# Fetching four active adapters by register-offset transfers instead of selecting them by matmuls

## The reference, cut to what matters

```
y = einsum('bth,oh->bto', x, W_base) + b_base
A = lora_A[active]                                   # 4 of 16, each 8 x 1024
Bm = lora_B[active]                                  # 4 of 16, each 1024 x 8
z = einsum('bth,erh->bter', x, A)
contribs = einsum('bter,eor->bteo', z, Bm) * SCALING
logits = (einsum('bth,eh->bte', x, router_W) + router_b)[..., active]
alpha = softmax(log(domain_prior[active] + EPS) + logits)
return y + einsum('bteo,bte->bto', contribs, alpha)
```

## Time and profile before

| | |
|---|---|
| median of 3 runs | 1496.22 us (1495.15 to 1497.36) |
| the profiled execution | 1493.93 us |
| its span | 1492.1 us |
| granted TensorE clock, mean | 0.998 |
| busy: PE, DVE, ACT, POOL | 98%, 67%, 48%, 31% |
| DMA queue of SyncE | 144.96 MB, 35.9% of 16 engines |

### The profile page before, as it was taken

One profiled execution on the slowest core, in us unless ns is written; L12 is line 12 of the kernel. 1 busy time (PEld: TensorE's weight loads), 2 busy tenths in 40 slices (PEclk: granted clock), 3 DMA queues, 4 the chain that ended last, 5 costly groups with the idle time before them and its releaser, 6 DMA issues.

```text
span 1492.1 us, 28269 instructions
## 1 busy us (share of the span) xinstructions
PE 1465.0 (98%) x9647; PEld 1376.2 (92%) x9647; DVE 994.3 (67%) x2367; ACT 722.3 (48%) x1618; POOL 462.1 (31%) x537
## 2 busy tenths in 40 slices
PE   6999999999999999999999999999999999999999
PEld 4889898989988988898879999999999999999998
DVE  8756576666565655555676777677677677677674
ACT  5544455545544444554444454454454454454452
POOL 3133233223323323332412332332332332332230
PEclk9999999999999999999999999999999999999999
DMA  6443423442342343234423334334324324324322
GB/s 133 112 104 106 115 79 92 113 114 86 85 113 71 99 113 99 77 106 112 139 101 100 89 80 112 90 79 112 94 75 112 96 72 112 97 72 112 99 70 71
DMA packets 54644, 145.99 MB, mean 98 GB/s; under 512 B 17265, under 2 KB 19761, under 8 KB 54594
## 3 DMA queue, kind: packets, MB, share of 16 engines
q1 hardware_dynamic: 53904, 144.96, 35.9%
q10 hardware_dynamic: 690, 0.37, 0.1%
HBM read 111.75 MB, written 33.55 MB: 97 GB/s over the span
## 4 chain that ended last, share of the span: by engine, by line
PE 94%; DVE 3%; issue 1%; DMA 0%; POOL 0%; ACT 0%; SPq 0%; POOLq 0%; DVEq 0%; ACTq 0%
PE bank L1579 48%; PE bank L1406 13%; PE bank L1408 13%; PE bank L1407 13%; PE bank L1739 4%; PE bank L1611 1%; PE bank L1600 1%; PE bank L1644 1%; PE bank L1673 0%; DMA ends<-in_x_dram 0%; DVE win L1144 0%; DVE mtmp L1143 0%; PE bank L1756 0%; PE bank L1662 0%; DVE fw_l L1138 0%
## 5 line engine op out<-in xcount | busy, mean ns | idle before, releaser
L1579 PE MATMUL bank<-fw_h,ct_h 128*128 128x354 f32 (+2 forms) x1256 | 448.9, 357 | 0.8 <-DVE xout L1109 0.8
L1579 PE MATMUL bank<-fw_l,ct_h 128*128 128x354 f32 (+2 forms) x1256 | 444.9, 354 | 0.0
L1579 PE MATMUL bank<-fw_h,ct_l 128*128 128x354 f32 (+2 forms) x1256 | 443.2, 353 | 0.0
L401 POOL COPY conv_buf<-edge 128x4 f32 (+1 forms) x128 | 21.6, 197 | 852.5 <-DVE tw L1240 838.6
L1579 PEld LDWEIGHTS bank<-fw_h,ct_l 128*128 128x128 f32 x1256 | 236.3, 188 | 21.4
L1579 PEld LDWEIGHTS bank<-fw_h,ct_h 128*128 128x128 f32 x1256 | 236.8, 189 | 17.7 <-DVE ct_l L1264 0.9
L1579 PEld LDWEIGHTS bank<-fw_l,ct_h 128*128 128x128 f32 x1256 | 236.8, 189 | 15.5
L392 POOL TENSOR_TENSOR d_l<-d_f,d_h 128x512 fp32r<-128x512 f32 x128 | 154.9, 1210 | 106.2 <-ACT d_h L605 106.1
L1406 PE MATMUL bank<-d_h,tw 128*128 128x256 f32 x640 | 181.5, 284 | 0.3 <-DVE beta L945 0.3
L386 POOL TENSOR_TENSOR d_f<-xraw 128x512 f32<-128x512 f32 x128 | 170.0, 1351 | 35.1 <-DMA xraw<-in_x_dram 19.2
L1408 PE MATMUL bank<-d_h,tw 128*128 128x256 f32 x640 | 180.7, 282 | 0.0
(11 more groups left out here) (254 smaller groups left out, 3128.9 us busy)
## 6 DMA issues: line engine op xcount, KB each, us to landing
xraw<-in_x_dram SPq DMA_DIRECT2D x32, 512.0 KB, 6.5
xres<-in_x_dram SPq DMA_DIRECT2D x32, 512.0 KB, 4.3
x_dram<-xout SPq DMA_DIRECT2D x32, 512.0 KB, 3.0
xraw<-x_dram SPq DMA_DIRECT2D x32, 512.0 KB, 6.5
xres<-x_dram SPq DMA_DIRECT2D x32, 512.0 KB, 4.4
xraw<-in_x_dram SPq DMA_DIRECT2D x32, 511.5 KB, 7.8
xraw<-x_dram SPq DMA_DIRECT2D x32, 511.5 KB, 7.9
out_dram<-xout SPq DMA_DIRECT2D x31, 512.0 KB, 2.9
```

What stands on the lines that cost most here:

```text
L1579: last = mm(ffn_ps[e][:, 0:cols.stop - cols.start], ctf((ct_h, ct_h, ct_l)[part], k), (fw_h, fw_l, fw_h)[part][:, k, cols], start=k == beg ...
```

## The change

The indices are clamped as before and also written as integers (`act_c`, step 5). At the turns of pairs 9 to 12 (`GATHER` = 9), SyncE reads one index each into a register and issues three transfers with that register as offset: the expert's A (8 rows of `a_in`), its router row (a ninth kind of row, `a_in` rows 32 to 35), and its B (64 columns of `b_in`, 1024 pieces of 32 bytes). The loads of all sixteen A, B and router rows go. Step 15 on TensorE keeps the small product `lsum` and has eight transposes of the 36 gathered rows; step 16 has eight transposes of B, which VectorE packs three times over at step 15 (`prep_pack`). `sel`, `prep_b_turn`, `prep_b_turned` and `prep_between` go; `prep_rows` on VectorE moves from step 17 to 16 and `prep_base` from 16 to 17. In layer 1 the turn of pair 2 moves into the loop.

```
 def load_lora():
     for dst, src in ((act_i[:, :], a["L1_ffn_active"].unsqueeze(0).broadcast_to([P, E_ACT])),
-                     (a_in, a["L1_ffn_lora_A"].rearrange("e r h -> (e r) h")),
-                     (b_in, a["L1_ffn_lora_B"].rearrange("e (p g) r -> p e g r", g=CHUNKS)),
                      (rb_in[:, :], a["L1_ffn_router_b"].unsqueeze(1)),
                      (pr_in[:, :], a["L1_ffn_domain_prior"].unsqueeze(1))):
         sp.dma_start(dst, src).then_inc(zs["lora_in"], 16)
+
+def gather(e):
+    sp.wait_ge(zs["chosen_ready"], 1)
+    v = sp.value_load(act_c[0:1, e:e + 1], min_val=0, max_val=E_TOT - 1)
+    sp.dma_start(a_in[R * e:R * e + R, :], a["L1_ffn_lora_A"][bass.ds(v, 1)].rearrange("o r h -> (o r) h")
+                 ).then_inc(zs["gathered"], 16)
+    sp.dma_start(a_in[ZR + e:ZR + e + 1, :], a["L1_ffn_router_W"][bass.ds(v, 1)]).then_inc(zs["gathered"], 16)
+    sp.dma_start(b_in[:, 64 * e:64 * e + 64].rearrange("p (g r) -> p g r", g=CHUNKS),
+                 a["L1_ffn_lora_B"][bass.ds(v, 1)].rearrange("o (g p) r -> (o p) g r", g=CHUNKS)
+                 ).then_inc(zs["gathered"], 16)
...
-turn(2, not n)
-if not n:
-    load_lora()
-with sp.Fori(3, NPAIR) as j:
-    turn(j)
+if n:
+    with sp.Fori(2, NPAIR) as j:
+        turn(j)
+else:
+    turn(2, True)
+    load_lora()
+    with sp.Fori(3, GATHER) as j:
+        turn(j)
+    for e in range(E_ACT):
+        turn(GATHER + e)
+        gather(e)
+    with sp.Fori(GATHER + E_ACT, NPAIR) as j:
+        turn(j)
...
-nc.scalar.dma_start(r_in, a["L1_ffn_router_W"]).then_inc(zs["lora_late"], 16)
...
 def prep_pack():
-    dve.wait_ge(zs["lora_in"], 16 * 5)
-    v.tensor_copy(b_pack, b_in.rearrange("p e g r -> p g e r")).then_inc(zs["pack_ready"], 1)
+    dve.wait_ge(zs["gathered"], 16 * 3 * E_ACT)
+    for i in range(3):
+        last = v.tensor_copy(b_pack[:, :, i, :, :], b_in.rearrange("p (e g r) -> p g e r", e=E_ACT, g=CHUNKS))
+    last.then_inc(zs["pack_ready"], 1)
...
 def prep_base(link):
-    dve.wait_ge(zs["lora_late"], 32)
+    dve.wait_ge(zs["lora_late"], 16)
+    dve.wait_ge(zs["bb_acc"], 1)
...
+def prep_rows():
+    pe.wait_ge(zs["sel_ready"], 1)
+    pe.wait_ge(zs["gathered"], 16 * 3 * E_ACT)
+    mm(bank[6][:, 256:256 + E_ACT], lsum[:, :], sel16[:, :], start=True, stop=True)
+    for k in range(CHUNKS):
+        pos = slice(256 * (k // 2) + k % 2, 256 * (k // 2) + 256, 2)
+        last = nc.tensor.transpose(bank[7][:, 64 * k:64 * k + NZ], a_in[:, pos], ident[0:NZ, 0:NZ])
+    last.then_inc(zs["ar_acc"], 1)
...
 def prep_b_rows():
     pe.wait_ge(zs["ar_ready"], 1)
-    for g in range(2):
-        last = mm(bank[6 + g][0:96, :], sel[:, :, :, :].rearrange("p g e r -> p (g e r)"),
-                  b_t[:, 512 * g:512 * g + 512], start=True, stop=True)
+    pe.wait_ge(zs["pack_ready"], 1)
+    for g in range(CHUNKS):
+        last = nc.tensor.transpose(bank[6 + g // 4][0:3 * ZR, (g % 4) * P:(g % 4 + 1) * P],
+                                   b_part[:, 3 * ZR * g:3 * ZR * g + 3 * ZR], ident[:, :])
     last.then_inc(zs["bb_acc"], 1)
```

More of the change, by code:

```diff
@@ L52 @@
 PREP, PREPS = 2, 20
+GATHER = PREP + 7
 def half(p):
@@ L199, in build @@
         act_m = sb("act_m", [P, E_ACT])
[L200 to L205, removed]
+        act_c = sb("act_c", [P, E_ACT], I32)
+        pidx_i = sb("pidx_i", [P, 1], I32)
+        pidx = sb("pidx", [P, 1])
         sel16 = sb("sel16", [E_TOT, E_ACT])
@@ L213, in build @@
         b_part = win[1][:, 0:L]
-        b_pack = b_part.rearrange("p (g e r) -> p g e r", g=CHUNKS, e=E_TOT)
+        b_pack = b_part[:, 0:CHUNKS * 3 * ZR].rearrange("p (g i e r) -> p g i e r", g=CHUNKS, i=3, e=E_ACT)
         f_rows = [f_in[0], f_in[1], xres, xout]
-        a_in, r_in, bias_in = f_in[0][:, :], win[0][0:E_TOT, 0:L], win[0][96:97, 0:L]
-        b_in = f_in[1][:, :].rearrange("p (e g r) -> p e g r", e=E_TOT, g=CHUNKS)
-        b_t = f_in[1]
+        a_in, bias_in = f_in[0][0:NZ, :], win[0][96:97, 0:L]
+        b_in = f_in[1][:, 0:E_ACT * CHUNKS * R]
         gate = sb("gate", [P, 16])
@@ L249, in build @@
         zs = {k: sem(k) for k in (
[L250 removed]
+            "f_load0 f_load1 f_load2 f_load3 style_load style_acc pack_ready lora_in ident_made bias_row_moved ln_in ln_ready sel_ready chosen_ready gathered ar_acc "
             "ct_rest wk_side st_made down_made scales_made lora_late ar_ready bb_acc bb_ready z_acc logit_ready exp_ready zcat_ready zt_acc zt_ready gate_step sta_zero").split()}
@@ L367, in _ @@
             nc.gpsimd.iota(pidx_i[:, 0:1], [[0, 1]], base=0, channel_multiplier=1).then_inc(zs["ident_made"], 1)
-            nc.gpsimd.iota(rr_i[:, :, :], [[0, E_ACT], [1, R]], base=0, channel_multiplier=0).then_inc(zs["ident_made"], 1)
             for h in range(2):
@@ L374, in _ @@
             nc.gpsimd.memset(xraw[:, :, L:L + 2], 0.0).then_inc(zs["ident_made"], 1)
-            pool.wait_ge(zs["ident_made"], 5)
+            pool.wait_ge(zs["ident_made"], 4)
             nc.gpsimd.memset(sta[:, :, :], 0.0).then_inc(zs["sta_zero"], 1)
@@ L947, in prep_pack @@
             def prep_pack():
-                dve.wait_ge(zs["lora_in"], 16 * 5)
-                v.tensor_copy(b_pack, b_in.rearrange("p e g r -> p g e r")).then_inc(zs["pack_ready"], 1)
+                dve.wait_ge(zs["gathered"], 16 * 3 * E_ACT)
+                for i in range(3):
+                    last = v.tensor_copy(b_pack[:, :, i, :, :], b_in.rearrange("p (e g r) -> p g e r", e=E_ACT, g=CHUNKS))
+                last.then_inc(zs["pack_ready"], 1)
             def prep_chosen(link):
-                dve.wait_ge(zs["ident_made"], 4)
+                dve.wait_ge(zs["ident_made"], 3)
+                dve.wait_ge(zs["lora_in"], 16 * 3)
                 link(v.tensor_copy(act_f[:, :], act_i[:, :]))
@@ L958, in prep_chosen_2, with prep_log_in @@
             def prep_chosen_2(link):
[L959 to L965, removed]
+                v.tensor_copy(act_c[:, :], act_f[:, :]).then_inc(zs["chosen_ready"], 1)
+                link(v.tensor_copy(pidx[:, :], pidx_i[:, :]))
                 v.tensor_scalar(sel16[:, :], act_f[0:E_TOT, :], pidx[0:E_TOT, 0:1], None, ALU.is_equal)
[L968 to L971, removed]
+            def prep_log_in(link):
                 link(v.tensor_scalar(gate[0:E_TOT, 0:1], pr_in[:, :], PRIOR_EPS, None, ALU.add))
                 v.tensor_copy(gate[0:E_TOT, 1:2], gate[0:E_TOT, 0:1]).then_inc(zs["ln_in"], 1)
[L975 to L979, removed]
             def prep_prior(link):
@@ L992, in prep_rows, with prep_b_rows @@
                 v.tensor_copy(const4[:, :], bank[6][:, 256:256 + E_ACT]).then_inc(zs["ar_ready"], 1)
-            def prep_b_rows(link, g):
+            def prep_b_rows(link, i):
                 dve.wait_ge(zs["bb_acc"], 1)
[L997 to L1001, removed]
+                cols = slice(512 * i, 512 * i + 512)
+                v.tensor_copy(bb[0:64, cols], bank[6 + i][0:64, :])
+                link(v.tensor_copy(b_part[64:96, cols].bitcast(F32R), bank[6 + i][64:96, :]))
+                last = v.tensor_tensor(bb[64:96, cols], bank[6 + i][64:96, :], b_part[64:96, cols], ALU.subtract)
+                if i:
                     last.then_inc(zs["bb_ready"], 1)
             def prep_base(link):
-                dve.wait_ge(zs["lora_late"], 32)
+                dve.wait_ge(zs["lora_late"], 16)
+                dve.wait_ge(zs["bb_acc"], 1)
                 link(v.tensor_copy(bb[96:97, :], bias_in))
@@ L1054, in prep_behind_v @@
                     prep_prior(link)
+                elif i == 15:
+                    prep_pack()
                 elif i == 16:
+                    prep_rows(link)
+                elif i == 17:
                     prep_base(link)
-                elif i == 17:
-                    prep_rows(link)
                 elif i in (18, 19):
@@ L1073, in prep_behind_t @@
                     prep_kernels(ly, (3,))
-                elif i == 4:
-                    prep_pack()
                 elif i == 5:
@@ L1085, in prep_behind_t @@
                     prep_w3(ly, link)
-                elif i == 10:
-                    prep_selected(link)
                 elif i == 11:
-                    prep_selected_2(link)
+                    prep_log_in(link)
                 elif i == 12:
                     prep_bias(ly, link, 0)
-                    prep_b_turned(0)
                 elif i == PREPS:
@@ L1489, in prep_bias @@
                 last.then_inc(s["bias_acc"], 1)
[L1491 to L1508, removed]
-                    pos = slice(256 * (k // 2) + k % 2, 256 * (k // 2) + 256, 2)
[L1510 to L1515, removed]
+            def prep_rows():
[3 more added lines that the diff above has]
+                for k in range(CHUNKS):
+                    pos = slice(256 * (k // 2) + k % 2, 256 * (k // 2) + 256, 2)
+                    last = nc.tensor.transpose(bank[7][:, 64 * k:64 * k + NZ], a_in[:, pos], ident[0:NZ, 0:NZ])
+                last.then_inc(zs["ar_acc"], 1)
```

(8 more changed lines are left out.)

1 line of the change is left out of this document (removed).

## The result

The median went from 1496.61 us (1495.15 to 1497.36, 4 runs) to 1485.38 us (1484.12 to 1486.91, 4 runs): a ratio of 0.9931 with a 95% interval of 0.9919 to 0.9942, that is 8.7 to 12.1 us less. The forecast was 1485.6. The profiled execution took 1485.3 us, its span 1483.5.

The account below looks back on a forecast made before the run. TensorE, 94% of the span, was taken as the bound. The profiled 1493.93 us less 6.5 (TensorE work) and 4.1 (stall), gathers free, gives 1483.3, so median 1485.6; likeliest range 1484 to 1487.5, wider range 1483 to 1491; chance 0.64.

Parts of the forecast that it names:

- TensorE removed and added: TensorE, steps 15 to 17 and `prep_b_turn`: 8.63 us of work go, 2.15 us come, gain 6.5 us.
- eight 36-row transposes, 0.91: TensorE, new transposes of the gathered rows: 0.91 us added, priced from the six 64-row transposes.
- The B transposes, 0.89: TensorE, eight transposes of the packed B, 128 rows like `prep_b_turn`: 0.89 us added.
- Rival 4: TensorE: the sixteen transposes cost 0.35 us each, like the small matmuls; 1489.4 us, chance 0.04.
- The stall: Pair 3: TensorE's 2.7 us wait on `conv_buf` and 1.4 us of slow clock go with the big loads, gain 4.1 us.
- rival 1: Pair 3: tiny loads or a full queue still hold x, only the matmuls count; gain 6.5, 1489.7 us, chance 0.12.
- The gathers: Queue at pairs 9 to 12: register load and three issues delay x by 2.6 us, hidden, costing nothing.
- The slack: Pairs 9 to 12: x may land 3.0 us later per gather before TensorE waits, 0.4 us to spare.
- Rivals 2 and 3: Pairs 9 to 12: gathers make TensorE wait, 1488.0 to 1493.6 us (chance 0.12) or, as long as the old stall, 1502.0 (0.05).
- rival 2: Pairs 9 to 12: TensorE waits 0.6 us four times, 1488.0; with 1.4 us slow clock each, 1493.6; chance 0.12.
- VectorE and the rest: `prep_pack` at step 15, moved `prep_rows` and `prep_base`, one ScalarE load and GpSimd iota less: no effect on the time.
- The median: Whole kernel: profiled execution 1483.3 us, 2.3 us under the median of the runs, so median 1485.6 us.

Follow-up runs that it names:

- the last two runs: Changed kernel with step 15's eight transposes taking 64 rows instead of 36: 1486.08 us; changed kernel with them reading neighbouring columns: 1485.56 us.

## Why the prediction was right, by its steps

- **TensorE removed and added: gain 6.5, measured 5.94.** The mechanism held and the size is 0.5 us off. Of this, 0.33 are the term "eight 36-row transposes, 0.91": their pair was lengthened by 1.59 us, not 1.26, because it was priced by transposes that read neighbouring columns, and these read every second one (the last two runs; with neighbouring columns the pair is lengthened by 1.13, a little less than the price). 0.17 are `prep_b_turn`: its 0.89 us on the chain gave back 0.72, so work between pairs does not lengthen a pair by exactly its size on the chain; why was not looked into. The B transposes, 0.89, lengthened their pair by 0.93. Rival 4, transposes as dear as small matmuls, is refuted by 0.134 and 0.109 us against 0.35: one record of a 36-row transpose lasts 0.284 us, but they follow one another every 0.134.
- **The stall: gain 4.1, measured 4.14.** The wait and the slow clock went whole, and the pair takes 22.07 us, close to the 22.2 forecast. x was issued 2.6 us behind `load_res`, less than the 3.6 allowed for. Moving the loads alone gives this part and putting them back takes it away; rival 1, only the matmuls count, is what the run with the loads back shows: 1490.1, where the rival said 1489.7.
- **The gathers: nothing, measured nothing.** x is 2.0 us late, forecast 2.6, but by two errors of opposite sign: the register load costs 0.98 to 1.53 us, not 0.65, and the three issues 1.3 us, not 1.95; that these nearly cancel is luck. The Trainium skill, "DMA: Bandwidth & Descriptors", section "Latency and other measured facts", has at least about 600 ns for a `tensor_load`; the trace agrees with the "at least", with 0.98 to 1.53 us, small instructions included. GpSimd waited 0.2 to 1.4 us in the two profiles, where 1 to 2 were forecast, and not at the fourth gather.
- **The slack.** From GpSimd's plain start the prediction had 275.9 - 273.71 = 2.2 us; the two runs with more gathers in a turn show 2.3 both times (7.84 - 5.50, 2.82 - 0.52). Counted from the issue of x the slack was mis-sized: 3.0 us were forecast, 0.4 of them to spare, and the same two runs show about 4 us free (4.6 - 0.52, 9.6 - 5.50), so with x 2.0 us late about 2 are to spare. Rivals 2 and 3 are therefore real mechanisms, but their threshold lies about 1 us further out than the prediction had it, and the change stays well below it: with two gathers a turn about 1 us is lost by the marks, with four 7 to 8. The price put on a small overrun was too high: a wait of 0.52 us brought no slow clock, where rival 2 had 1.4 us in its worse form.
- **VectorE and the rest: nothing, measured nothing** on TensorE: the pairs of steps 15 and 16 are longer by about the size of `lsum` and their transposes (1.59 and 0.93 us, of which 1.38 and 0.87 stand on the chain), that of step 17 by nothing.
- **The median.** 1485.6 was 1483.3 plus the 2.3 us by which the profiled execution lay under the median. The execution profiled after took 1485.3, not 1483.3, and the marks show that 2.0 us of it are the opening, which varies by nearly as much between executions that do not differ there; taking the offset into the median was right. That the median came within 0.2 us of the forecast is in part luck: the marks give 10.1 us of the 10.6 forecast, the medians differ by 11.2, and the runs of one kernel spread by more than a microsecond to either side.

## What to carry to other kernels

When a selection by matmul is replaced by a transfer with a register offset, count two places: the work that leaves the bounding engine, at its distance between marks, and what the old bulk load did to the loads queued behind it, which here was 40% of the gain. Small transfers ahead of a critical load are priced by the slack of that load: find how late it may land, add up register load and issues on the queue's engine, and spread them over as many turns as keep each below it. And price a transpose by a row with the same access to its columns, not by one with about the same number of rows.

## What the runs showed of the hardware

- A transpose on TensorE that reads every second fp32 column took 0.134 us against 0.077 for neighbouring columns, with 36 rows; 64 rows in place of 36 changed nothing (0.137). The Trainium skill, "SBUF — State Buffer", section "Door 1: The DMA port swizzle", says of accesses in general that fp32 may be read with a stride of up to four elements for free. The trace differs for this read, at stride two, and it decides.
- A register load of one index with its small instructions kept SyncE for 0.98 to 1.53 us, by the gaps ahead of the four gathers with and without it.
- A TensorE wait of 0.52 us left the granted clock at 1.00; waits of 2.7 and 5.5 us were followed by 0.50.
- The opening of the kernel varies by 1.8 us between executions of kernels that do not differ there (72.19 to 73.97 us to the mark of pair 2), while the 430 us behind that mark repeat within 0.1 us in the two profiles of the changed kernel.
